# A mask correction of the grouped feed-forward in four bands of 32 rows, with a new table of turns

## The chip, the core and the metric

The kernel runs on one core of one Trainium2 chip. The core has a matrix engine (PE; PEld is its weight loading), a vector engine (DVE), a scalar engine for activations (ACT), a general engine (POOL) and a queue engine that starts most of the transfers (SP). The metric is the device time of one execution, in microseconds (us). Everything is computed in float32.

## The reference

Input `x` has 64 x 64 tokens of 256 numbers, 4096 rows. Two layers are computed, each with a mixer, a cross attention on `ctx_512` and a feed-forward, all with a residual. The change lies in the last of the six parts, the grouped feed-forward of layer 1:

```python
def _L1_ffn_ref(hidden_states, gate_w, mask_up_w, gate_proj_w, up_proj_w, down_proj_w, inv_map):
    scores = jax.nn.softmax(x @ gate_w.T, axis=-1)                  # 64 experts
    topk_w, topk_idx = jax.lax.top_k(scores, 8)
    w_e = jnp.zeros((N, E), x.dtype).at[jnp.arange(N)[:, None], topk_idx].add(topk_w)
    flat = w_e[:, inv_map]                                          # 8 groups of 8
    scalar = flat.sum(-1)
    soft = jax.nn.softmax(jnp.where(flat == 0, NEG_INF, flat), axis=-1)
    xg = x[:, None, :] + jnp.einsum('ngi,ghi->ngh', soft, mask_up_w)
    g = jnp.einsum('ngh,gih->ngi', xg, gate_proj_w)                 # 176 wide, 8 groups
    u = jnp.einsum('ngh,gih->ngi', xg, up_proj_w)
    a = jax.nn.silu(g) * u
    d = jnp.einsum('ngi,ghi->ngh', a, down_proj_w)
    y = jnp.einsum('ng,ngh->nh', scalar, d)
```

The product of `xg` with the gate and up weights is split: `x` times the weights of the group, plus `soft` (8 numbers of each token and group) times `mask_up_w` multiplied by the weights beforehand. The second summand is called the correction here.

## The kernel before

The 4096 rows are 32 tiles of 128; two tiles are a block, so there are 16 blocks. Each part of the network is a stage with one small program (a generator) for each engine and block: `s1` (state space mixer), `s2` and `s3` (latent cross attention), `shared`, `experts` and `more` (mixture of experts, with rows sorted through memory), `s4` (recurrent mixer of layer 1), `s5` (its cross attention), `s6` (the grouped feed-forward, with `ffn` once ahead of it to prepare weights). Where a program says `yield`, its engine may pass to another program. `weave` decides: every piece of every program has a due time, `START` of its stage and block plus its entry in `TURNS`, and the pieces of an engine are written down in the order of these times. That order is fixed when the program is built; each engine then runs its list strictly in order and waits at semaphores. The due times do nothing else.

From about the middle of the program, one period of the list holds `s6` of block n, `s5` of block n + 1 and `s4` of block n + 2. `s4` and `s5` have one set of buffers each, so they run block after block; `s6` has two (`arena` and `BIG`).

The accumulators of PE are eight banks (`ps`). A stage takes them in turn from a ring: `s4` and `s5` from banks 0 to 3 (ring "s5"), `s6` and `ffn` from banks 4 to 7 (ring "s6"). Before PE may write a bank it waits for the step that emptied it last.

What `s6` does with a block, by the lines of the profile:

- L1926 transposes the normalised rows `h` (made by ACT at L872); ACT copies them to `hT` (L2080). L1936 computes the scores, DVE and ACT make a softmax and pick the eight largest (L2012 to L2029), L1944 transposes them, L1953 applies `inv_map`. DVE and ACT make the softmax of each group, which ends with L2052, and L1961 transposes the result; DVE copies it to `soT` (L2055).
- For each of the two tiles and for g = 0 to 3, PE computes two groups, g and g + 4: L1972 multiplies `hT` with the 352 columns of a group (two matmuls for each of the two groups, so four), L1978 adds the correction, one matmul for each group. `soT` has 64 rows, 8 for each group; the correction of group g + 4c takes the band of 32 rows 32c to 32c + 31, of which only 8 count, since `MG` (64 rows x 8 groups x 352) is zero elsewhere. ACT takes the silu of the gate half (L2094), DVE multiplies it with the up half and the group's weight into `AG` (L2064).
- L1988 transposes `AG` in three banks, ACT copies it (L2102), L1997 multiplies with the down weights (11 matmuls), DVE adds the result to `X` (L2069), which frees the bank, and SP stores it (L2112).

Each matmul is issued as two instructions by the compiler, so the four of L1972 are eight in the trace and the two of L1978 are four.

In `s4`, DVE runs two scans (L1524, later L1542 and L1544), a chain of products (L1549 to L1555), a reciprocal (L1557) and a product (L1561); PE multiplies the result with the output weights (L1492), DVE adds that to `X` (L1564). POOL then gathers the rows of the next block (L1611). In `s5`, L1678 are transposes, L1692 and L1706 matmuls on bands of 32 rows that use four banks of ring "s5" at a time, L1717 products whose output is 32 rows wide, L1726 transposes; POOL adds the result to `X` (L1841).

## Time and profile before

| | us |
|---|---|
| median of 3 runs | 2146.43 (2146.39 to 2149.85) |
| the profiled execution's own time | 2144.75 |
| its span, first to last instruction | 2143.0 |
| PE busy | 2039.6 (95%) |
| DVE busy | 1370.2 (64%) |
| ACT busy | 993.2 (46%) |
| POOL busy | 641.0 (30%) |
| mean granted clock of PE | 0.989 |

The span is read in three parts: the first layer up to about 1250 us with the expert stages at its end, the even stretch from 1252 to 2047 us in which `s4`, `s5` and `s6` repeat every 59.1 us, and the end, in which `s6` of the last blocks runs alone.

### The profile page before, as it was taken

What the parts mean: (1) busy time and instruction counts of PE and PEld (TensorE: products, weight loads), DVE (VectorE), ACT (ScalarE), POOL (GpSimd) and SP (SyncE); (2) the same over time, 40 slices, a digit from 0 to 9 for tenths busy, and PEclk for the clock granted to TensorE, in tenths of its full rate; (3) what the DMA queues carried; (4) which work ended last, traced back from release to release, by engine and by line L of the source; (5) the groups of instructions that cost most, each with busy time, mean ns of one, the idle gap of its engine ahead of it and who ended that gap; (6) DMA issues with size and microseconds to landing.
All of it is one profiled execution on the core that took longest, in us unless ns stands there. A gap on an engine that the chain in (4) does not pass through costs nothing.

```text
span 2143.0 us, 40150 instructions
## 1 busy us (share of the span) xinstructions
PE 2039.6 (95%) x15072; PEld 1574.9 (73%) x15072; DVE 1370.2 (64%) x3453; ACT 993.2 (46%) x1974; POOL 641.0 (30%) x988
## 2 busy tenths in 40 slices
PE   6999999999999999999878799999999999999998
PEld 5888888888888778888656566666666666666665
DVE  3677777777778424333256687777777777777631
ACT  1455555555545433333234354455445445454542
POOL 1334443343344620000132332333332333333200
PEclk9999999999999999999899899999999999999999
DMA  5300150000001343222211100000000000000000
GB/s 166 119 14 23 32 194 14 9 21 14 9 21 50 124 150 126 84 80 77 82 49 31 57 23 26 25 26 26 26 13 16 26 26 26 24 26 25 16 6 8
DMA packets 82347, 102.18 MB, mean 48 GB/s; under 512 B 17128, under 2 KB 68464, under 8 KB 81648
## 3 DMA queue, kind: packets, MB, share of 16 engines
q1 hardware_dynamic: 76016, 82.84, 12.1%
q0 software_dynamic: 6144, 16.79, 2.4%
q8 instruction: 125, 2.05, 0.4%
q14 instruction: 62, 0.51, 0.1%
HBM read 62.90 MB, written 36.70 MB: 46 GB/s over the span
## 4 chain that ended last, share of the span: by engine, by line
PE 89%; DVE 4%; ACT 3%; issue 2%; another core or an unknown queue 1%; POOL 1%; DMA 1%; SPq 1%; ACTq 0%; POOLq 0%; DVEq 0%
PE ps L1972 15%; PE ps L1384 9%; PE ps L1997 7%; PE ps L366 7%; PE ps L725 5%; PE ps L782 5%; PE ps L1978 5%; PE ps L1482 4%; PE ps L415 2%; PE ps L1375 2%; PE ps L1988 2%; PE ps L1286 2%; PE ps L1706 2%; PE ps L1692 1%; PE ps L1717 1%
## 5 line engine op out<-in xcount | busy, mean ns | idle before, releaser
L1384 PE MATMUL ps<-BIG,arena 128*128 x912 | 220.4, 390 | 25.1 <-DVE arena L1417 8.6
L1384 PEld LDWEIGHTS ps<-BIG,arena 128*128 128x128 f32 x912 | 170.4, 194 | 56.8 <-issue 35.6
L1420 DVE COPY arena<-ps 128x512 f32<-128x512 f32 x114 | 78.4, 689 | 140.7 <-PE ps L1384 135.4
L1972 PE MATMUL ps<-EARLY,arena 128*128 128x352 f32 x512 | 166.6, 468 | 0.0
L1972 PE MATMUL ps<-EARLY,BIG 128*128 128x352 f32 x512 | 166.5, 468 | 0.0
L366 PE MATMUL ps<-arena,EARLY 128*128 128x256 f32 x640 | 150.7, 385 | 0.0
L1440 ACT ACTIVATE arena<-ps,BIG 128x128 f32<-128x128 f32 x304 | 85.9, 373 | 138.5 <-PE ps L1375 132.8
L1972 PEld LDWEIGHTS ps<-EARLY,BIG 128*128 128x128 f32 x512 | 92.7, 190 | 56.2 <-issue 12.2
L1972 PEld LDWEIGHTS ps<-EARLY,arena 128*128 128x128 f32 x512 | 92.7, 190 | 55.8 <-issue 11.2
L1217 POOL DMA_INDIRECT rows_by_slot<-back,posi x64 | 62.5, 976 | 232.2 <-DMA back<-rows_by_token 214.5
L366 PEld LDWEIGHTS ps<-arena,EARLY 128*128 128x128 f32 x640 | 119.0, 192 | 16.9 <-issue 2.3
L1611 POOL DMA_INDIRECT arena<-results_by_slot,posi x64 | 63.0, 985 | 137.1 <-DVE X L1564 110.8
L468 DVE SCALAR_TENSOR_TENSOR arena<-ps,c_convw,arena 128x252 f32<-128x252 f32 (+2 forms) x192 | 91.4, 476 | 6.8
L2064 DVE SCALAR_TENSOR_TENSOR BIG<-BIG,ps 128x176 f32<-128x176 f32 x128 | 45.0, 393 | 74.6 <-ACT BIG L2094 74.6
L1623 POOL TENSOR_SCALAR arena<-arena,om 128x256 f32<-128x256 f32 x96 | 51.6, 551 | 136.2 <-ACT arena L1575 136.2
L2064 DVE SCALAR_TENSOR_TENSOR arena<-arena,ps 128x176 f32<-128x176 f32 x128 | 45.0, 393 | 71.0 <-ACT arena L2094 71.0
L1482 PE MATMUL ps<-arena,c_w_kvro 128*128 128x256 f32 x384 | 87.7, 385 | 0.0
L1997 PE MATMUL ps<-BIG 128*128 128x256 f32 x352 | 79.6, 382 | 6.4 <-ACT BIG L2102 4.0
L1997 PE MATMUL ps<-BIG,arena 128*128 128x256 f32 x352 | 79.5, 382 | 5.4 <-issue 2.9
L1799 ACT ACTIVATE arena<-ps 128x512 f32<-128x512 f32 x128 | 66.5, 602 | 38.5 <-PE ps L1706 38.4
L570 POOL TENSOR_TENSOR arena<-arena 128x512 f32<-128x512 f32 x32 | 40.6, 1268 | 143.5 <-DVE arena L495 143.5
L1771 DVE TENSOR_REDUCE arena<-ps 128x8 f32<-128x512 f32 x128 | 80.1, 679 | 1.5 <-PE ps L1692 1.4
(404 smaller groups left out, 4823.3 us busy)
## 6 DMA issues: line engine op xcount, KB each, us to landing
arena<-rows_by_slot SPq DMA_DIRECT2D x38, 256.0 KB, 2.7
results_by_slot<-arena SPq DMA_DIRECT2D x38, 256.0 KB, 2.1
rows_by_slot<-zrow SPq DMA_DIRECT2D x3, 2304.0 KB, 15.5
BIG<-in_moe_w SPq DMA_DIRECT2D x3, 1792.0 KB, 9.9
X<-in_x SPq DMA_DIRECT2D x8, 512.0 KB, 4.9
rows_by_token<-BIG SPq DMA_DIRECT2D x16, 256.0 KB
arena<-rows_by_token SPq DMA_DIRECT2D x16, 256.0 KB
back<-rows_by_token SPq DMA_DIRECT2D x16, 256.0 KB
```

The source lines that it names most:

```text
L366: m = e.matmul(ps[:, f * 256:f * 256 + 256], w_in[:, c, c0 + f * P:c0 + f * P + P], L.hT[:, c, :], start=c == 0, stop=c == 1, skip_group_c ...
L468: m = e.scalar_tensor_tensor(c3[:, :, d:64], s3[:, :, 0:64 - d], convw[:, f, 3 - d:4 - d], c3[:, :, d:64], ALU.mult, ALU.add)
L725: m = e.matmul(ps[:, f * 256:f * 256 + 256], Aw[:, c, (2 * g + f) * P:(2 * g + f) * P + P], L.hT[:, c, :], start=c == 0, stop=c == 1, skip ...
L782: m = e.matmul(ps[:, 0:256], L.qT[:, q, i * P:i * P + P], Bw[:, q, :], start=q == 0, stop=q == 7, skip_group_check=True)
L1384: m = e.matmul(ps[:, q * 256:q * 256 + 256], src[:, q, c * P:c * P + P], BIG[:, bass.ds(pe_reg[ex.A.j0 + 2 * n + q] + (w0 + c * 256), 256) ...
L1440: m = e.activation(dst[:, q, c * P:c * P + P], bank.of(k(name))[:, q * 256 + c * P:q * 256 + c * P + P], func, bias=BIG[:, bass.ds(act_reg ...
L1482: m = e.matmul(ps[:, f * 256:f * 256 + 256], kvro[:, j, c, f * P:f * P + P], L.mx[j][:, c, :, :], start=c == 0, stop=c == 1, skip_group_ch ...
L1771: e.tensor_reduce(L.hq[:, i, :, 2 * q:2 * q + 2, 8], bank.of(k(f"s{i}{q}"))[:, :].rearrange("p (g k l) -> p g k l", g=4, k=2), AX, ALU.max ...
L1972: e.matmul(ps[:, 0:352], L.hT[:, q, ts], WG[:, q, gs], start=q == 0, stop=False, skip_group_check=True)
L1978: e.matmul(bank.of(k(f"u{i}{g}{c}"))[:, 0:352], L.soT[rows, ts], MG[rows, gs], start=False, stop=True, skip_group_check=True).then_inc(*ba ...
L1997: m = e.matmul(ps[:, 0:256], L.AT[:, q, :], WD[:, q, :], start=q == 0, stop=q == 10, skip_group_check=True)
L2064: e.scalar_tensor_tensor(L.AG[:, gg * 176:gg * 176 + 176], L.sg[:, c, :], L.s8[0][:, 8 * i + gg:8 * i + gg + 1], bank.of(k(f"u{i}{g}{c}")) ...
```

## The change

1. **Four bands.** `soT` gets 128 rows: four bands of 32 of which 16 count. Band q holds group q in its first 8 rows and group q + 4 in the next 8. Where one tensor operation on DVE wrote the group softmax (L2052), four smaller ones (L2064 of the new file) now write it into a zeroed buffer `so` in this layout. `MG` becomes 128 rows x 2 x 352, and the host lays out `mw` and `mg` to match.
2. **Four groups a batch.** For each tile there are two batches, b = 0 and 1. A batch takes all four banks of the ring "s6" and waits until all four are empty, then issues the four corrections (on four different bands, one bank each, now as the first summand), then the four groups' eight matmuls with `hT`, with a `yield` between groups. Before, the matmuls with `hT` came first and the correction second.
3. **Small groups in the other ring.** The five small results of `s6` (transposed h, scores, transposed weights, `inv_map`, transposed softmax) take banks from ring "s5" in place of "s6".
4. **`sg`** has four buffers in place of two, so ACT may be four groups ahead of DVE.
5. **A new table.** All entries of `START` and `TURNS` are replaced, for every stage and engine, so the lists of all five engines change throughout the program. Two lines of about ninety are shown.

```diff
-    "s6": {"dve": (0.41, 8.37, 8.42, 20.05, 24.63, 27.76, 32.04, 36.9, 37.82, 46.6, 50.4, 64.45, 67.43, 71.67, 75.47,
+    "s6": {"dve": (1.55, 9.29, 10.85, 16.29, 25.86, 28.47, 36.17, 40.9, 42.35, 53.48, 53.48, 66.81, 70.55, 72.67,
...
-        MG = BIG[0:64, 2816:5632]
+        MG = BIG[:, 2816:3520].rearrange("p (b n) -> p b n", b=2)
...
-            ps = bank.take("s6", k("so"), s6v, n, "soT")
+            ps = bank.take("s5", k("so"), s6v, n, "soT")
             e.wait_ge(*s6v.at(n, "so"))
             e.wait_ge(*bank.empty(k("so")))
             for i in range(TB):
-                m = e.transpose(ps[0:64, i * P:i * P + P], L.fl[:, i, :], ident)
+                m = e.transpose(ps[:, i * P:i * P + P], L.so[:, i, :], ident)
             m.then_inc(*bank.made(k("so")))
             for i in range(TB):
                 ts = slice(i * P, i * P + P)
-                for g in range(4):
+                for b in range(2):
                     yield
-                    for c in range(2):
-                        gs = slice((g + 4 * c) * 352, (g + 4 * c) * 352 + 352)
-                        ps = bank.take("s6", k(f"u{i}{g}{c}"), s6v, n, f"ag{i}{g}{c}")
-                        e.wait_ge(*bank.empty(k(f"u{i}{g}{c}")))
-                        for q in range(2):
-                            e.matmul(ps[:, 0:352], L.hT[:, q, ts], WG[:, q, gs], start=q == 0, stop=False,
-                                     skip_group_check=True)
-                    if i == 0 and g == 0:
+                    if i == 0 and b == 0:
                         e.wait_ge(*s6v.at(n, "soT"))
-                    for c in range(2):
-                        rows, gs = slice(32 * c, 32 * c + 32), slice((g + 4 * c) * 352, (g + 4 * c) * 352 + 352)
-                        e.matmul(bank.of(k(f"u{i}{g}{c}"))[:, 0:352], L.soT[rows, ts], MG[rows, gs], start=False, stop=True,
-                                 skip_group_check=True).then_inc(*bank.made(k(f"u{i}{g}{c}")))
+                    for q in range(4):
+                        g = 4 * b + q
+                        bank.take("s6", k(f"u{i}{g}"), s6v, n, f"ag{i}{g}")
+                        e.wait_ge(*bank.empty(k(f"u{i}{g}")))
+                    for q in range(4):
+                        rows, ps = slice(32 * q, 32 * q + 32), bank.of(k(f"u{i}{4 * b + q}"))
+                        e.matmul(ps[:, 0:352], L.soT[rows, ts], MG[rows, b, :], start=True, stop=False,
+                                 skip_group_check=True)
+                    for q in range(4):
+                        if q:
+                            yield
+                        g = 4 * b + q
+                        ps = bank.of(k(f"u{i}{g}"))
+                        for c in range(2):
+                            m = e.matmul(ps[:, 0:352], L.hT[:, c, ts], WG[:, c, g * 352:g * 352 + 352], start=False,
+                                         stop=c == 1, skip_group_check=True)
+                        m.then_inc(*bank.made(k(f"u{i}{g}")))
...
-            e.tensor_tensor(g3(L.fl), g3(L.fl), bc(L.s8[3]), ALU.mult).then_inc(*sig("so"))
+            for i in range(TB):
+                for b in range(2):
+                    m = e.tensor_tensor(L.so[:, i, :].rearrange("p (q w) -> p q w", q=4)[:, :, 8 * b:8 * b + 8],
+                                        L.fl[:, i, 32 * b:32 * b + 32].rearrange("p (q w) -> p q w", q=4),
+                                        L.s8[3][:, 8 * i + 4 * b:8 * i + 4 * b + 4].unsqueeze(2).broadcast_to([P, 4, 8]), ALU.mult)
+            m.then_inc(*sig("so"))
```

In the new file the lines of `s6` are: corrections L1977, matmuls with `hT` L1985, transposes of `AG` L1996, down projection L2005, transposed h L1928, softmax transposes L1963; on DVE the four small products L2064, `soT` L2070, the products into `AG` L2078, the sum into `X` L2083.

How the list of PE changes, one stretch in the middle of the program, from the recurrent mixer's first projections (L1482) on. Before:

```order
L1482 MATMUL ps<-arena,c_w_kvro 128x256 x12
L1997 MATMUL ps<-BIG,arena 128x256 x11
L1961 MATMUL ps<-c_ident,BIG 64x128 x2
L1706 MATMUL ps<-arena 128x256 x8
L1972 MATMUL ps<-EARLY,BIG 128x352 x4
L1978 MATMUL ps<-BIG 128x352 x2
L1972 MATMUL ps<-EARLY,BIG 128x352 x4
L1978 MATMUL ps<-BIG 128x352 x2
L1678 MATMUL ps<-c_ident,arena 128x128 x4
L1717 MATMUL ps<-arena 32x256 x8
L1972 MATMUL ps<-EARLY,BIG 128x352 x4
L1978 MATMUL ps<-BIG 128x352 x2
```

The same stretch in the changed kernel:

```order
L1482 MATMUL ps<-arena,c_w_kvro 128x256 x4
L1996 MATMUL ps<-c_ident,arena 128x128 x3
L1482 MATMUL ps<-arena,c_w_kvro 128x256 x8
L2005 MATMUL ps<-BIG,arena 128x256 x11
L1706 MATMUL ps<-arena 128x256 x8
L1963 MATMUL ps<-c_ident,BIG 128x128 x2
L1678 MATMUL ps<-c_ident,arena 128x128 x4
L1977 MATMUL ps<-BIG 128x352 x4
L1985 MATMUL ps<-EARLY,BIG 128x352 x4
L1717 MATMUL ps<-arena 32x256 x8
L1985 MATMUL ps<-EARLY,BIG 128x352 x4
L1706 MATMUL ps<-arena 128x256 x8
```

The corrections now stand ahead of the first matmul with `hT`, four together, and only one step of transposes (L1678) lies between the transposed softmax (L1963) and them; before, L1706 and four matmuls with `hT` lay there. After the last row shown the next four corrections follow at once.

How the list of DVE changes at the same place, from the last product of the group softmax on. Before:

```order
L2052 TENSOR_TENSOR arena<-arena 128x128
L1542 SCALAR_TENSOR_TENSOR arena<-arena 128x520
L1544 SCALAR_TENSOR_TENSOR arena<-arena 128x520
L2055 COPY arena<-ps 64x256
L2069 TENSOR_TENSOR X<-ps,X 128x256
L2064 SCALAR_TENSOR_TENSOR arena<-arena,ps 128x176 x4
L1549 TENSOR_TENSOR arena<-arena 128x512
L1551 TENSOR_TENSOR arena<-arena 128x512
L1553 TENSOR_TENSOR arena<-arena 128x512
L1555 SCALAR_TENSOR_TENSOR arena<-arena 128x512
L1557 RECIPROCAL arena<-arena 128x512
L1561 TENSOR_TENSOR arena<-arena 128x512
```

The four products of `AG` (L2064) stand between the copy to `soT` and the chain L1549 to L1561.

DVE at the same place in the changed kernel, from the four small products (L2064) on:

```order
L2064 TENSOR_TENSOR BIG<-BIG 128x4x8 x4
L1542 SCALAR_TENSOR_TENSOR arena<-arena 128x520
L1544 SCALAR_TENSOR_TENSOR arena<-arena 128x520
L2083 TENSOR_TENSOR X<-ps,X 128x256
L2070 COPY BIG<-ps 128x256
L1549 TENSOR_TENSOR arena<-arena 128x512
L1551 TENSOR_TENSOR arena<-arena 128x512
L1553 TENSOR_TENSOR arena<-arena 128x512
L1555 SCALAR_TENSOR_TENSOR arena<-arena 128x512
L1557 RECIPROCAL arena<-arena 128x512
L2078 SCALAR_TENSOR_TENSOR BIG<-BIG,ps 128x176 x4
L1561 TENSOR_TENSOR arena<-arena 128x512
```

The copy to `soT` (L2070) stands behind the sum into `X`, and all products of the first batch into `AG` (L2078) stand behind the chain L1549 to L1557.

SP's list changes too. At the start of the program it was, before:

```order
L2116 DMA X<-in_x 128x4x256
L598 DMA arena<-in_wqr 64x768
L598 DMA arena<-in_wkr 64x256
L598 DMA arena<-in_wkcq 96x2x512
L598 DMA arena<-in_wq 128x1024
```

The list begins with `x`, and the loads of L598 follow at once. SP at the start of the changed kernel:

```order
L2141 DMA c_ident<-in_ident 128x128
L2141 DMA EARLY<-in_w_in 128x2568
L2141 DMA c_nscale<-in_nscale 128x2
L2141 DMA c_convw<-in_convw 128x16
L2141 DMA c_convb<-in_convb 128x4
```

The tables and the first layer's weights now come first; the loads of L598 and the rest of `x` stand behind them.

## Rows read from the trace of the kernel before

**Rows 1.** Two stretches: length, busy time (instructions) by engine, PE's clock, DMA.
```profile
1000.00:1250.00 250.00, 204.47 (x1234) 153.72 (x1233) 139.53 (x251) 91.39 (x220) 68.90 (x93) 0.91 0.17 56
1252.00:2047.00 795.00, 783.60 (x5887) 539.04 (x5889) 592.28 (x1302) 400.29 (x763) 245.83 (x357) 1.00 0.07 23
```

**Rows 2.** PE in time order: start us, length, line, count, [idle before it].
```profile
1637.44 0.38 PE L1961 MATMUL ps<-c_ident,BIG 128*64 128x128 f32 x2
1637.76 1.15 PE L1706 MATMUL ps<-arena 32*128 32x256 f32 x16
1638.83 2.63 PE L1972 MATMUL ps<-EARLY,BIG 128*128 128x352 f32 x8
1641.40 0.86 PE L1978 MATMUL ps<-BIG 32*128 32x352 f32 x4
1642.19 2.63 PE L1972 MATMUL ps<-EARLY,BIG 128*128 128x352 f32 x8
...
1645.54 0.66 PE L1678 MATMUL ps<-c_ident,arena 128*128 128x128 f32 x4
1646.13 1.07 PE L1717 MATMUL ps<-arena 128*32 128x256 f32 x16
...
1654.70 1.99 PE L1492 MATMUL ps<-c_w_kvro,arena 128*128 128x256 f32 x8
...
1669.47 0.66 PE L1926 MATMUL ps<-c_ident,arena 128*128 128x128 f32 x4 [0.99 <-ACT arena L872]
...
1686.78 0.55 PE L1988 MATMUL ps<-c_ident,BIG 128*128 128x128 f32 x3
1687.16 5.35 PE L1482 MATMUL ps<-arena,c_w_kvro 128*128 128x256 f32 x24
...
1697.10 0.38 PE L1961 MATMUL ps<-c_ident,arena 128*64 128x128 f32 x2
```

**Rows 3.** DVE in time order, the end of the softmax and the chain of `s4`.
```profile
1645.99 0.71 DVE L2064 SCALAR_TENSOR_TENSOR BIG<-BIG,ps 128x176 f32<-128x176 f32 x2 [2.64 <-ACT BIG L2094]
1646.62 0.68 DVE L1549 TENSOR_TENSOR arena<-arena 128x512 f32<-128x512 f32 x1
...
1653.60 0.69 DVE L1561 TENSOR_TENSOR arena<-arena 128x512 f32<-128x512 f32 x1
...
1689.91 1.23 DVE L1524 TENSOR_TENSOR_SCAN arena<-td,arena 128x520 f32<-128x520 f32 x1
...
1695.31 0.89 DVE L2052 TENSOR_TENSOR arena<-arena 128x128 f32<-128x128 f32 x1
...
1700.44 0.39 DVE L2055 COPY arena<-ps 64x256 f32<-64x256 f32 x1
1700.76 0.40 DVE L2069 TENSOR_TENSOR X<-ps,X 128x256 f32<-128x256 f32 x1
```

**Rows 4.** Two short steps of DVE one behind the other, in time order.
```profile
1724.94 0.17 DVE L429 TENSOR_SCALAR small<-small 128x2 f32<-128x2 f32 x1
1725.02 0.16 DVE L808 TENSOR_SCALAR small<-small 128x2 f32<-128x2 f32 x1
```

**Rows 5.** POOL in time order, beside the end of the softmax.
```profile
1694.87 1.19 POOL L1631 TENSOR_TENSOR arena<-arena 128x512 f32<-128x512 f32 x1 [2.07 <-DVE arena L1537]
1696.01 1.23 POOL L1634 TENSOR_TENSOR arena<-arena 128x512 f32<-128x512 f32 x1
```

**Rows 6.** From L1492 to the next block's h, in another period, on PE.
```profile
1714.35 1.99 PE L1492 MATMUL ps<-c_w_kvro,arena 128*128 128x256 f32 x8
...
1728.56 0.66 PE L1926 MATMUL ps<-c_ident,BIG 128*128 128x128 f32 x4
```

**Rows 7.** ACT in the same period, where h is made.
```profile
1726.62 1.09 ACT L872 ACTIVATE BIG<-X,small 128x256 f32<-128x256 f32 x2 [6.22 <-POOL small L882]
```

**Rows 8.** PE at the start of the program, in time order.
```profile
11.90 2.82 PE L609 MATMUL ps<-arena 64*96 64x64 f32 x16 [11.90 <-DMA c_ident<-in_ident]
...
22.08 3.68 PE L628 MATMUL ps<-arena 96*128 96x64 f32 x16 [5.46 <-DVE arena L645]
```

229 lines of the change are left out of this document (117 added, 112 removed), and 9 rows, old and new, of the table START.

## The prediction, made before the run

> **What bounds the kernel now.** The first view is the busy time of the engines over the whole span, shown in the table above: PE has work for 95% of it. The second is the same by stretches [rows 1]. From 1252 to 2047 us PE is busy 783.6 of 795 us, DVE 592.3; PE is idle 11.4 us, some 0.85 in each period of 59.1. So in this stretch only less time of PE's own instructions can shorten the span, and only as long as the change makes PE wait no longer than it saves. From 1000 to 1250 us PE is busy 204.5 of 250, with a granted clock of 0.91, and 45.5 us are idle: a stretch of waits. The third view is PE in order of time [rows 2]: there the price of a correction can be read. The fourth is DVE and POOL in order of time [rows 3 to 5], which shows when the inputs of the corrections are ready.
>
> **Fewer, wider corrections.** A step of eight instructions of L1972 and four of L1978 takes 1642.19 - 1638.83 = 3.36 us [rows 2]. The eight alone: from the start of L1482 to that of L1961 stand 24 instructions of L1482 and 22 of L1997 with 256 columns each, 46 in 1697.10 - 1687.16 = 9.94 us, so 0.216 each, 0.297 for 352 columns, 2.38 for eight. That leaves 0.98 for a visit to the bands. Two passes of 352 columns are 0.59 of it, the other 0.39 goes to changing over and back. The visit already has its two bands side by side; one behind the other, four instructions would be 1.19 alone, more than the 0.79 between L1978's start and the next line's start (1641.40 to 1642.19).
>
> That four bands can also run side by side is shown by L1706: 16 instructions of 256 columns on four bands stand 1638.83 - 1637.76 = 1.07 us before the next line [rows 2]. One behind the other they would take 16 x 0.216 = 3.5. So I take 0.98 for a visit of four corrections too. A block has eight visits before and four after: 3.9 us less. In places a visit now follows L1706 directly, whose changeover it shares, as it sometimes did; I take off 0.3 and have 3.6 for a block, 58 us for 16 blocks. The bounds of the visit's price are 0.98 and, if bands ran two at a time, 0.98 + 0.59 = 1.57.
>
> As a sentence apart: the Trainium skill, TensorEngine Tiling (Array Packing), section Gotcha 1: PSUM Pressure, says that row tiles running at once need different banks of PSUM; by that rule the new code's four banks a batch are the price of the overlap, and L1706, whose row agrees with it, pays it already. What the rule says against this change is in the next part, worked out from rows.
>
> **What the four banks cost.** The batch needs `soT` and all four banks of its ring before its first correction; before, matmuls with `hT` on two banks came first. I lay the new order of PE over the times of the old. Zero is the start of L1482.
>
> *First batch.* DVE before, after zero: L1524 starts at +2.75 (1689.91 - 1687.16), L2055 at +13.28, and `soT` is ready at +13.67 [rows 3]. PE reached the correction 9.94 + (1641.40 - 1637.44) = 13.9 after zero [rows 2]: no slack. Now four small products replace L2052 (0.89). Their price no row has: the nearest rows are two short steps that start 0.08 apart and last 0.17 [rows 4], so about 0.45 for four; 1.3 if each takes what a step of DVE with PSUM takes (about 0.3). I take 0.45, since each writes 32 numbers a row. The first of two sums into `X` now stands ahead of the copy: 0.32 from L2055 to L2069's start [rows 3] is the pitch of such steps. So `soT` is ready at 13.67 - 0.44 + 0.32 = 13.55. PE now arrives at 9.94 + 0.38 (three transposes moved in, 1687.16 - 1686.78) + 1.07 (L1706) + 0.32 (L1963) + 0.59 (L1678) = 12.3 [rows 2]. It waits 1.3, which before was covered by a step of L1972.
>
> *Second batch.* It needs the first batch's four products out of PSUM, and these now stand behind the chain L1549 to L1557 and ahead of L1561: 1653.60 - 1646.62 = 6.98 for the chain, then 4 x 0.315 (1646.62 - 1645.99 for two) [rows 3]. From 13.55 that gives 21.8. PE arrives after 0.98 + 2 x 2.38 + 1.0 (L1717) + 1.07 (L1706) = 7.8 to 8.1, at 21.6: a wait of 0.2, but nothing is left over. Behind it 0.8 and, in most blocks, two groups of 1.19 stand ahead of L1492, which starts at 25.1. It was 9.94 + (1654.70 - 1637.44) = 27.2 before [rows 2].
>
> *To the next h.* From L1492 it went 14.2 to L1926 on PE, and 1726.62 + 1.09 - 1714.35 = 13.4 to the end of `h` on ACT [rows 6, 7]. PE's own work there is now 13.0 at most, so the chain over DVE, POOL and ACT decides: 13.5, with a wait of 0.5 to 1.0 (0.99 stood there in one period before [rows 2]).
>
> *From there to zero.* 1687.16 - 1669.47 = 17.7 before [rows 2]. Off go three steps of 3.36 and the moved transposes 0.38; on come two visits of 0.98 and eight groups of 1.19, 11.5 together, and an estimated 0.3 for the last batch, whose four banks must be emptied by ACT and DVE (one product, 0.315) while only short transposes cover it: 19.1.
>
> The period is then 25.1 + 13.5 + 19.1 = 57.7 in place of 59.1: 1.4 less. Of the 3.6 won, 2.2 return as waits. Some 14 periods are of this kind, 19.6 us; in the last two blocks, where `s6` has nothing beside it, the four-bank wait is bare, and I take 1 us for both together.
>
> **Small groups in the other ring, four buffers `sg`.** Both only move waits; no instruction is added. The ring of `s5` had free turns beside them, and ACT ahead of DVE helps where DVE is late. Nothing, within 0.2 a block either way.
>
> **Copies and host layout.** `L1963` puts out 128 rows in place of 64 and L2070 copies 128 in place of 64: columns set the time, the same. Zeroing `so` is twice in the whole program, on POOL (30% busy in the table).
>
> **The new table, first layer and experts.** I followed the orders of PE, DVE, ACT and POOL from the start to 1250 us: the places with short cover (expert stages) are as many and of about the same size in both. I take nothing. The bounds: better than half of the 45.5 us idle [rows 1] gone, -25; as much as a third more, +15. At the start of SP's list, `c_ident` and the first weights now come first, and the loads of L598 stand behind fifteen others. PE's start at 11.90 may slip to 16 or 18, but the 5.46 us which L628 waited for L645 go with it, since it is then loaded in between [rows 8]. Nothing, within 4. The stores of `s5` and `s6` come later on SP; nobody waits for them but the end, and they are short beside the last block's.
>
> **The sum.** 2144.75 - 19.6 - 1 = 2124.2 for the profile's own time. The median of the runs is 1.7 above that execution, so 2126 is the median forecast.
>
> **Rivals.**
>
> A. *The forecast*, 2126: visits at 0.98, 2.2 a block back as waits. Its own spread, from the products at 1.3 (0.9 a block later, 12 us) to waits of half the size (15 us less): 2111 to 2138.
>
> B. *The waits are covered.* If DVE gets to `soT` and the products earlier, since `s4` and `s5` now run at another offset, only the sum of PE's work counts: 58 less, 2088. For it: DVE is free a quarter of the time [rows 1]. Against it: `soT` had no slack before, and the chain from L1524 on has not become shorter.
>
> C. *The new table removes waits of the expert stages*: half of the 45.5 us more, 2126 - 24 = 2102. Against it: the orders look alike there.
>
> D. *Slower: the chain on DVE decides the period.* The place is the end of the softmax and L1549 to L1561. L2052 took 0.89 for 128 numbers a row, where L2069, for 256, took 0.40 [rows 3]; POOL's L1631 and L1634 ran beside it, 1.19 and 1.23 [rows 5]. If each small product or the chain L1549 to L1555 is held by one of these, DVE comes 1.5 to 2.4 later to `soT` and to the products of the first batch. PE has no slack at either, so every microsecond beyond the forecast's counts: from 1.4 on the gain is gone, at 2.2 the period is 59.9, and 14 periods make it 2157.
>
> As a sentence apart: the Trainium skill, SBUF, State Buffer, section Who interferes with whom, says that DVE and GpSimd share a pair of ports under an exclusive lock; by that, D's wait is real, and the long L2052 beside POOL fits it, though it happened before the change as well and is in the old period.
>
> E. *The bands run two at a time.* 0.59 more a visit, 2.4 a block, of which about 0.7 is taken from the waits that stand behind a visit (the second batch, L1926): period 57.7 + 1.7 = 59.4, 14 x 1.7 = 24 more than A, 2150. Against it stands L1706 [rows 2].
>
> **How the numbers follow.** A 0.52, B 0.18, C 0.10, D 0.13, E 0.07. The range leaves out the far side of B and D: from 2086, just under B, to 2152, which takes in E and the mild part of D. A change under 0.2% (4.3 us) is about what a measurement can't tell from none: faster 0.77 (A, B and C, 0.80, less 0.03 for A with the first layer's bound of +15 on top), same 0.10 (E and that), slower 0.13 (D).
>
> **What would show it.** In the changed profile: L1977, eight instructions, 0.8 to 0.9 us before L1985, and not 1.4 (A against E). PE idle about 1.3 us ahead of L1977, put down to DVE's L2070, and a little ahead of the second, put down to L2078 (A against B). A period of 57.7 between starts of L1482's groups; 59.9 with L2064 or L1555 stretched beside L1631 and L1634 is D, 55.5 is B. Idle time of PE from 1000 to 1250 of 45 us; 22 is C. The forecast is wrong above all if the table shifts `s4` against `s6` so that the softmax ends earlier than the old times say.

## The result, and the profile after it

The changed kernel is slower. Its median is 2165.2 us (8 runs, 2155.2 to 2172.6) beside 2147.1 for the kernel before on the same chip, ratio 1.0083 (95% interval 1.0070 to 1.0095). The forecast was 2126 with a range up to 2152, so both the size and the sign are wrong. The profiled execution has a span of 2163.0 us, 20.0 more than before.

The page of the changed kernel, busy time by engine, answers to the table ahead of the prediction:

```profile
PE 2012.1 (93%) x15072; PEld 1572.0 (73%) x15072; DVE 1388.7 (64%) x3501; ACT 1005.2 (46%) x1974; POOL 645.4 (30%) x990
```

PE has 27.5 us less work and the span is 20 us longer, so PE stands idle 47 us more. The stretches of [rows 1] in the changed kernel (length, busy time of PE, PEld, DVE, ACT, POOL, PE's clock, DMA):

```profile
1000.00:1250.00 250.00, 203.56 (x1262) 157.47 (x1262) 144.63 (x252) 92.39 (x227) 55.38 (x75) 0.95 0.17 54
1252.00:2047.00 795.00, 746.63 (x5732) 526.39 (x5730) 589.29 (x1323) 405.97 (x754) 257.61 (x371) 0.99 0.08 23
```

In the even stretch idle time of PE went from 11.4 to 48.4 us. The starts of L1482's sixteen groups tell where the 20.0 us arise. The fourth group, the first beside `s6`, starts at 1286.7 in place of 1272.6: 14.1 us are lost ahead of it. From there to the sixteenth it is 720.1 in place of 710.0: 10.1 more. From the sixteenth to the end it is 156.2 in place of 160.4: 4.2 less.

One period of PE in the changed kernel, in order of time (start us, length, line, count, [idle before it]), answers to [rows 2]:

```profile
1707.36 1.99 PE L1482 MATMUL ps<-arena,c_w_kvro 128*128 128x256 f32 x8
...
1719.72 0.41 PE L1963 MATMUL ps<-c_ident,arena 128*128 128x128 f32 x2 [0.76 <-ACT arena L1799]
1720.21 0.63 PE L1678 MATMUL ps<-c_ident,arena 128*128 128x128 f32 x4
1721.59 0.87 PE L1977 MATMUL ps<-BIG,arena 32*128 32x352 f32 x8 [0.75 <-DVE arena L2070]
1722.39 2.63 PE L1985 MATMUL ps<-EARLY,arena 128*128 128x352 f32 x8
1724.95 1.07 PE L1717 MATMUL ps<-arena 128*32 128x256 f32 x16
1725.95 2.63 PE L1985 MATMUL ps<-EARLY,arena 128*128 128x352 f32 x8
1728.52 1.15 PE L1706 MATMUL ps<-arena 32*128 32x256 f32 x16
1729.68 0.87 PE L1977 MATMUL ps<-BIG,arena 32*128 32x352 f32 x8
...
1732.95 1.89 PE L1492 MATMUL ps<-c_w_kvro,arena 128*128 128x256 f32 x8
...
1742.04 5.02 PE L2005 MATMUL ps<-BIG,arena 128*128 128x256 f32 x22 [1.42 <-ACT arena L2115]
1747.14 0.66 PE L1928 MATMUL ps<-c_ident,BIG 128*128 128x128 f32 x4
...
1757.59 0.87 PE L1977 MATMUL ps<-BIG,arena 32*128 32x352 f32 x8 [0.28 <-DVE arena L2078]
...
1766.51 1.99 PE L1482 MATMUL ps<-arena,c_w_kvro 128*128 128x256 f32 x8
```

Three things are to be seen. First, eight instructions of L1977, on four bands, hold PE for 1722.39 - 1721.59 = 0.80 us; four of L1978, on two bands, held it 0.79 in [rows 2]. The four bands do run side by side. Second, the waits named in the prediction are there (L1977 behind L2070, and 0.28 behind L2078), with one that it did not have: 1.42 before L2005, on the copies L2115 of ACT. In the twelve periods from the fourth group to the sixteenth this wait is 1.17 to 1.91, 20.2 us in all. Third, this period, 59.15 us, is as long as one of before. Longer ones come from the clock. Two neighbouring periods, by the same columns as above, and then the place in another period where the clock fell:

```profile
1407.00:1468.00 61.00, 57.28 (x436) 40.43 (x435) 44.82 (x101) 30.64 (x58) 19.50 (x28) 0.97 0.06 18
1468.00:1527.00 59.00, 55.73 (x435) 39.17 (x434) 44.66 (x101) 30.73 (x58) 19.51 (x28) 1.00 0.07 19
```

```profile
1897.36 0.41 PE L1963 MATMUL ps<-c_ident,BIG 128*128 128x128 f32 x2 [0.76 <-ACT arena L1799]
...
1899.16 0.87 PE L1977 MATMUL ps<-BIG 32*128 32x352 f32 x8 [0.69 <-DVE BIG L2070]
1899.97 4.33 PE L1985 MATMUL ps<-EARLY,BIG 128*128 128x352 f32 x8
```

Eight instructions of L1985 took 4.33 in place of 2.63: part of them ran at 1.2 in place of 2.4 GHz, after two waits close together. Five of twelve periods have a fall of the clock, at about 1.6 us each; the kernel before has none between 1252 and 2047 (its clock is 1.00 in [rows 1]). The falls have two places. Two of the five (1542 and 1900 us) stand behind these two waits; the other three (1323, 1443 and 1982 us) begin inside L2005, just behind its own wait of 1.9. A second execution of the changed kernel, `after_again`, has seven, five at the first place and two at the second.

### The profile page after: what moved, and what is told of

It is laid out like the page before. It is cut to its first block, busy times and chain, and to the rows that moved or that the text cites. A ratio compares the mean times of both kernels' runs of the same rounds, so it can differ in the third digit from the quotient of the medians.

```text
span 2163.0 us, 40298 instructions
## 1 busy us (share of the span) xinstructions
PE 2012.1 (93%) x15072; PEld 1572.0 (73%) x15072; DVE 1388.7 (64%) x3501; ACT 1005.2 (46%) x1974; POOL 645.4 (30%) x990
## 3 DMA queue, kind: packets, MB, share of 16 engines
q8 instruction: 126, 2.06, 0.4%
## 4 chain that ended last, share of the span: by engine, by line
PE 73%; DVE 16%; ACT 4%; issue 3%; POOL 2%; another core or an unknown queue 1%; DMA 1%; SPq 0%; ACTq 0%; POOLq 0%; DVEq 0%
PE ps L1985 15%; PE ps L1384 9%; PE ps L366 6%; PE ps L725 4%; PE ps L782 4%; PE ps L2005 3%; PE ps L1977 2%; PE ps L1375 2%; PE ps L415 2%; PE ps L1482 2%; PE ps L1286 2%; PE ps L1996 2%; PE ps L1692 1%; DVE arena L1527 1%; PE ps L1717 1%
## 5 line engine op out<-in xcount | busy, mean ns | idle before, releaser
L1384 PEld LDWEIGHTS ps<-BIG,arena 128*128 128x128 f32 x912 | 168.8, 192 | 59.6 <-issue 38.7
L1985 PE MATMUL ps<-EARLY,BIG 128*128 128x352 f32 x512 | 169.1, 475 | 0.0
L1985 PE MATMUL ps<-EARLY,arena 128*128 128x352 f32 x512 | 166.1, 468 | 0.0
L1611 POOL DMA_INDIRECT arena<-results_by_slot,posi x64 | 63.3, 988 | 310.7 <-DVE X L1564 169.4
L1985 PEld LDWEIGHTS ps<-EARLY,BIG 128*128 128x128 f32 x512 | 94.5, 193 | 63.2 <-issue 22.4
L1985 PEld LDWEIGHTS ps<-EARLY,arena 128*128 128x128 f32 x512 | 92.9, 190 | 61.7 <-issue 19.8
L366 PEld LDWEIGHTS ps<-arena,EARLY 128*128 128x128 f32 x640 | 120.6, 194 | 20.3 <-issue 4.2
L1217 POOL DMA_INDIRECT rows_by_slot<-back,posi x64 | 62.6, 978 | 126.7 <-DMA back<-rows_by_token 81.2
L2108 ACT ACTIVATE BIG<-ps 128x176 f32<-128x176 f32 x128 | 39.4, 317 | 123.5 <-PE ps L1985 123.2
L2005 PE MATMUL ps<-BIG 128*128 128x256 f32 x352 | 83.0, 394 | 12.2 <-ACT BIG L2115 10.4
L2005 PE MATMUL ps<-BIG,arena 128*128 128x256 f32 x352 | 81.2, 387 | 11.9 <-ACT arena L2115 11.9
L1482 PE MATMUL ps<-arena,c_w_kvro 128*128 128x256 f32 x384 | 91.7, 391 | 0.0
L2005 PEld LDWEIGHTS ps<-BIG 128*128 128x128 f32 x352 | 68.4, 197 | 24.0 <-ACT BIG L2115 12.3
L2108 ACT ACTIVATE arena<-ps 128x176 f32<-128x176 f32 x128 | 39.1, 317 | 99.6 <-PE ps L1985 99.4
L2005 PEld LDWEIGHTS ps<-BIG,arena 128*128 128x128 f32 x352 | 67.3, 193 | 23.1 <-ACT arena L2115 13.9
```

Source lines behind the costliest of these rows:

```text
L366: m = e.matmul(ps[:, f * 256:f * 256 + 256], w_in[:, c, c0 + f * P:c0 + f * P + P], L.hT[:, c, :], start=c == 0, stop=c == 1, skip_group_c ...
L1384: m = e.matmul(ps[:, q * 256:q * 256 + 256], src[:, q, c * P:c * P + P], BIG[:, bass.ds(pe_reg[ex.A.j0 + 2 * n + q] + (w0 + c * 256), 256) ...
L1482: m = e.matmul(ps[:, f * 256:f * 256 + 256], kvro[:, j, c, f * P:f * P + P], L.mx[j][:, c, :, :], start=c == 0, stop=c == 1, skip_group_ch ...
L1985: m = e.matmul(ps[:, 0:352], L.hT[:, c, ts], WG[:, c, g * 352:g * 352 + 352], start=False, stop=c == 1, skip_group_check=True)
L2005: m = e.matmul(ps[:, 0:256], L.AT[:, q, :], WD[:, q, :], start=q == 0, stop=q == 10, skip_group_check=True)
L2108: e.activation(L.sg[:, g % 4, :], bank.of(k(f"u{i}{g}"))[:, 0:176], ACT.Silu).then_inc(*sig(f"sg{i}{g}"))
```

## The experiments

Each group below ran on one chip together with the kernel before, and each of the five groups on another chip. That kernel took 2147.1, 2147.8 and 2150.9 us in three groups, and 2131.6 and 2131.5 in two others. I call these the slower and the faster condition; whether it is the chip or something about it that changes, no run here tells. The result above is of the slower condition. Ratios are always to the kernel before in the same group.

### Which part of the program loses: the first pair, a faulty one

The idea was to cross the tables: old turns up to the first `s6` with the new `s6`, and the other way round.

```
START/TURNS of s1, s2, s3, prod, first, x, tables, scatter, shared, experts, more, ffn; START of s4[0:2], s5[0]: from the other kernel
all later START: shifted by 201.96
```

> The changed kernel, but with the old table for every stage up to the end of the first layer, the first two blocks of s4, the first of s5, and ffn; from the first s6 on the lists are those of the changed kernel. Theory (two thirds of the loss lie in the new table ahead of s6, not in the four bands): the fourth group of L1482 starts near 1273 us in place of 1286.7, and the time is about 13 us under the changed kernel's, 2152. Rival (the first layer came out late by its clock in that one execution, or the loss is made by the batches): within 4 us of the changed kernel, 2161 to 2169.

> The counterpart: the kernel before, with the new table for the same stages, and its own lists from the first s6 on. Theory: the new table ahead of s6 costs the same here, so about 13 us over the kernel before, 2160. Rival: no change, 2147.

Measured: 2194.5 us (ratio 1.0230, 1.0209 to 1.0251) and 2189.0 (1.0195, 1.0175 to 1.0215). Both are far slower than either kernel. The fourth group of L1482 comes at 1310.6 and 1315.3 us, 38 and 29 us later than in the kernel whose table stands ahead (1272.6 and 1286.7). About 20 of this arise between the first and the third group (distances 75.2 and 72.6 us, and 78.0 and 72.0, in place of 67.3 and 62.6 in the kernel before and 64.9 and 63.2 in the changed one), most of the rest already ahead of the first. The cross was bad: blocks 0 and 1 of `s4` and block 0 of `s5` lie among the expert stages, and had the turns of the one table with the starts of the other. Neither the theory nor the rival is tested by it. It says only that a mismatch there costs 30 to 40 us, and that from the fourth group on each kernel keeps its own periods (60.2 on average with the new `s6`, 59.2 with the old).

### Covering the wait for soT, and doubling the visits

`cover` issues the matmuls with `hT` of two groups ahead of the four corrections:

```diff
-   take and wait for four banks; four corrections; hT for g0, g1, g2, g3
+   wait for two banks; hT for g0, g1; wait for soT and the other two banks; four corrections; hT for g2, g3
```

> The changed kernel with another order inside a batch: the matmuls with hT of the first two groups first, as the kernel before had it, then the four corrections, then the other two groups. Theory (the wait for soT ahead of the corrections costs 0.7 us a period by itself, and the falls of the clock that follow such waits cost another 1.7 in about every third): the wait before L1977 goes, the falls in the even stretch go, the period is 58.0 to 58.5, and the time is 14 to 20 us lower, 2146 to 2151. Rival (the chain L1549 to L1561 on DVE decides, so that the wait only moves to the second batch's banks): the period stays at 59.2 and the time within 5 us of the changed kernel less its clock falls, 2155 to 2165.

Measured: 2144.0 us (0.9988, 0.9977 to 0.9999). The place of the wait, in its PE list:

```profile
1471.61 2.53 PE L1979 MATMUL ps<-EARLY,arena 128*128 128x352 f32 x8
1474.08 0.87 PE L1990 MATMUL ps<-BIG,arena 32*128 32x352 f32 x8
...
1492.68 5.02 PE L2011 MATMUL ps<-BIG,arena 128*128 128x256 f32 x22 [1.87 <-ACT arena L2121]
```

The corrections (L1990 there) no longer wait, and the periods without a fall are 58.2 to 58.7, apart from two of 59.5 and 59.7 in which PE also waits 1.0 to 1.2 before L1928. Two falls are left in place of five, at 1730 and 1965 us, both inside L2011, behind its wait. So the theory held for the wait and nearly for the period; its falls did not all go, and the time is 2 us below its range. The rival, by which DVE's chain L1549 to L1561 would only take the wait over, fell. The wait on the copies of ACT (L2011 here is L2005) stayed, at 1.2 to 1.9.

`pairs` keeps everything but issues the corrections two and two:

```diff
-   C0 C1 C2 C3 | hT g0, g1, g2, g3
+   C0 C1 | hT g0, g1 | C2 C3 | hT g2, g3
```

> The changed kernel with its four corrections of a batch issued two and two: two ahead of the first two groups, two ahead of the others; banks, waits and tables unchanged, so eight visits to the bands a block in place of four. If a visit costs 0.98 alone (0.59 of passes and 0.39 of changing over), four more are 3.9 a block less what the waits take up: period 61.5 to 62.5, time 2200 to 2215. If what matters is the number of changes between bands and whole columns (eight more, at 0.1 each, and 0.59 of passes four times), 3.2 a block: 2195 to 2205. If four bands had run two at a time, only the changes are added, 1.6 a block: 2185.

Measured: 2213.3 us (1.0311, 1.0292 to 1.0330), periods without a fall of 62.0 to 62.6, apart from two of 63.8 with a longer wait before L1928. Against 59.2 that is about 3.0 for four more visits, but the wait before L2005 (L2006 here) has also fallen, from 1.2 to 1.9 down to 0.7 to 1.0 where no wait before L1928 stands. PE's busy time in a period without a fall rose by 3.5, from 55.6 to 59.1. The rows say how this is made up. A new visit next to another step on bands, such as the one behind L1717, adds the 0.79 that it holds PE. One between full-width steps also lengthens both neighbours: where L1985's twelve instructions held PE 1763.77 - 1760.12 = 3.65 in the changed kernel, the same twelve with a visit between them hold it 1597.91 - 1593.28 = 4.63 here, 0.98 more. Two of the four new visits are of each kind, 3.5 together. The first of the three expected outcomes held, in period and time: the prediction's 0.98 is right for a visit by itself, and one beside a step on bands costs 0.2 less. Two bands cost what four do.

### The cross again, joined cleanly

The first two blocks of `s4` and the first of `s5` now take the turns of the same table as their starts, so that the five lists are exactly those of one kernel up to the first step of `s6` and those of the other from there on.

```diff
-   (START[stage][n], TURNS[stage][engine], program(n))
+   (START[stage][n], (FIRST if n < {"s4": 2, "s5": 1}.get(stage, 0) else TURNS)[stage][engine], program(n))
```

> The changed kernel, whose five lists are those of the kernel before up to the first step of s6 (all stages of the first layer, s4 of blocks 0 and 1 and s5 of block 0 with their own old turns this time) and its own from there on. Theory (about 9 to 14 us of the loss lie in the new table ahead of s6): the fourth group of L1482 starts at 1273 to 1276 in place of 1286.7, the even stretch is as in the changed kernel (60.0 a period on average), time 2151 to 2156. Rival (only the clock of that execution made it late): 2161 to 2168.

> The counterpart: the kernel before with the changed kernel's lists up to the first step of s6, its own from there on. Theory: fourth group of L1482 at 1282 to 1287, then periods of 59.1, time 2156 to 2161. Rival: 2147.

Measured: 2129.6 us (0.9986, 0.9973 to 0.9999) and 2130.8 us (1.0000, 0.9985 to 1.0015). This group was the first in the faster condition. Neither theory nor rival foresaw it: the new `s6` is a little faster here, and the new table ahead costs nothing (fourth group of L1482 at 1265.0, with the old table 1270.2). The instructions last as long as before. What is shorter are waits: in `old_table_ahead`, which has the new `s6`, PE waits before L2005 0.36 us in every period, most periods are 58.0 to 58.2, and one fall of the clock is left, behind the wait for `soT`. The changed kernel itself was never run in the faster condition.

### Two numbers of the table, and one

`so_early` moves L1963 ahead of L1706 on PE and L2070 ahead of L2083 on DVE.

```diff
-   "s6": {"dve": (..., 28.47, 36.17, ...)    "pe": (..., 23.47, 35.14, ...)
+   "s6": {"dve": (..., 28.47, 33.3, ...)     "pe": (..., 23.47, 32.2, ...)
```

> The changed kernel with two numbers of the table moved: the transposes of the softmax (L1963) ahead of L1706 in PE's list, so that their bank in the ring of s5 is no longer one that ACT (L1799) has to empty first, and the copy to soT (L2070) ahead of the sum into X (L2083) in DVE's. Theory (both waits end at the same place, DVE's scans L1542 and L1544, which stand between the softmax and the copy): the 0.76 wait of L1963 goes, the wait of L1977 grows to 1.1 to 1.3, soT is ready 0.3 earlier, period 58.9, time 2160 to 2164. Rival (the wait of L1963 is a cost of the ring by itself): period 58.4, time 2152 to 2156.

Measured: 2191.7 us (1.0275, 1.0252 to 1.0298); theory and rival both wrong. Its waits of PE between 1300 and 2000 us (total, times, longest):

```profile
PE ps L1706 <- DVE arena L2070: 19.4, 6, 3.2
PE ps L1706 <- DVE BIG L2070: 16.1, 5, 3.2
PE ps L1678 <- ACT arena L1799: 8.0, 11, 0.7
```

L1706 needs all four banks of the ring, and one of them now holds the transposed softmax until L2070 has copied it. So with this group in `s5`'s ring there are only two orders. Behind L1706 it waits 0.76 for ACT to empty the first of the four banks; ahead of it, L1706 waits 3.2. So the move into the other ring does bring a wait of its own; what it costs in sum is tested by `cover_so` below.

`gather_late` moves POOL's gathers behind the sums into `X` and the powers for `h`.

```diff
-   "s4": {"pool": (-47.93, -30.43, ...
+   "s4": {"pool": (-30.9, -30.43, ...
```

> The changed kernel with one number of the table moved: POOL's four indirect gathers (L1611) behind the sums into X and the small powers for h (L879, L882), not ahead of them. Theory (while POOL issues the gathers, ACT answers PE's signals 0.4 us late and more, which makes the copies L2115 late and L2005 wait 1.2 to 1.9 us): the wait before L2005 falls to 0.4 or less, the period by 1.0 to 1.5, time 2148 to 2154, unless the next block of s4, whose rows come later, then waits for them. Rival (L2115 is late because of its place in ACT's list): the wait of L2005 stays at 1.2 or more and the time within 4 us of 2165.

Measured: 2263.8 us (1.0605, 1.0577 to 1.0633). It says nothing on its question. It ran in the faster condition, where L2005 waits 0.4 anyway, and the rows of `s4` came so late that PE waited up to 8.1 us in each period for DVE, before L1977.

### What differs between the conditions

In the faster condition the same step of the list can be laid beside the changed kernel's. ACT and POOL of the changed kernel, slower condition:

```profile
1739.31 0.60 ACT L1804 ACTIVATE arena<-ps 128x512 f32<-128x512 f32 x1 [1.75 <-PE ps L1717]
1740.03 1.96 ACT L2115 ACTIVATE arena<-ps 128x512 f32<-128x512 f32 x3
```

```profile
1737.25 0.97 POOL L1611 DMA_INDIRECT arena<-results_by_slot,posi  x1 [0.30 <-issue]
1738.52 0.95 POOL L1611 DMA_INDIRECT arena<-results_by_slot,posi  x1 [0.30 <-issue]
1739.77 0.95 POOL L1611 DMA_INDIRECT arena<-results_by_slot,posi  x1 [0.30 <-issue]
```

The same step with the same lists in `old_table_ahead`, faster condition, ACT, POOL and PE:

```profile
1711.93 0.60 ACT L1804 ACTIVATE arena<-ps 128x512 f32<-128x512 f32 x1 [1.15 <-PE ps L1717]
1712.48 1.47 ACT L2115 ACTIVATE arena<-ps 128x512 f32<-128x512 f32 x3
```

```profile
1711.73 0.95 POOL L1611 DMA_INDIRECT arena<-results_by_slot,posi  x1 [0.30 <-issue]
1712.98 0.95 POOL L1611 DMA_INDIRECT arena<-results_by_slot,posi  x1 [0.30 <-issue]
```

```profile
1710.79 1.07 PE L1717 MATMUL ps<-arena 128*32 128x256 f32 x16
...
1714.01 5.02 PE L2005 MATMUL ps<-BIG,arena 128*128 128x256 f32 x22 [0.36 <-ACT arena L2115]
```

PE starts L1717 at 1710.79 and ACT's L1804 follows 1.14 later, as the sixteen matmuls end. In the changed kernel L1717 starts at 1737.58 and L1804 only 1.73 later; the three copies then take 1.96 in place of 1.47. This happens while POOL issues the indirect gathers, and the gathers are the same in both conditions. The theory formed here: in the slower condition ACT and DVE answer PE late while POOL issues an indirect transfer, and the new table puts more work that PE waits for beside such transfers.

Two things in the traces make this theory sharper. First, it is PE's signals alone that come late. Beside the same gather, DVE answers ACT at once in the changed kernel:

```profile
1737.25 0.32 ACT L2108 ACTIVATE arena<-ps 128x176 f32<-128x176 f32 x1 [0.87 <-PE ps L1985]
1737.60 0.40 DVE L2078 SCALAR_TENSOR_TENSOR arena<-arena,ps 128x176 f32<-128x176 f32 x1 [0.79 <-ACT arena L2108]
```

ACT's step ends at 1737.57 and DVE's starts 0.03 later. Take the signals that ended a wait between 1252 and 2047 us, and the time of the semaphore event in this trace. 26 signals of PE come 0.4 to 1.27 us behind the recorded end of their matmul, two in each period (L1717, then L1726 or L1996), all beside the gathers or just behind them. All other signals of PE come within 0.05, and every signal of ACT and DVE within 0.02. In `old_table_ahead`, with the same gathers, no signal of PE is later than 0.05. The ends of matmuls are modelled in a profile, so whether PE works slower there or only signals later, these rows don't tell.

Second, the place matters within one execution. In the kernel before, slower condition, two neighbouring periods:

```profile
1659.74 1.08 POOL L1611 DMA_INDIRECT arena<-results_by_slot,posi  x1 [0.16 <-issue]
1660.31 5.01 PE L1997 MATMUL ps<-BIG 128*128 128x256 f32 x22 [0.36 <-ACT BIG L2102]
...
1717.36 1.08 POOL L1611 DMA_INDIRECT arena<-results_by_slot,posi  x1 [8.09 <-DVE X L1564]
1720.46 5.02 PE L1997 MATMUL ps<-BIG,arena 128*128 128x256 f32 x22 [0.86 <-ACT arena L2102]
```

Where the first gather starts 2.7 us behind L1717 (1657.06), the copies are nearly done and L1997 waits 0.36; where it starts 0.65 behind L1717 (1716.71), L1997 waits 0.86. In the changed kernel the first gather starts at 1735.86, 1.7 ahead of L1717, and the whole chain from L1717 to the copies lies beside the four.

The next group tests the theory by taking the indirect gathers away:

```diff
-   e.indirect_dma_start(y[:, i * 256:i * 256 + 256], None, ys_d[n // CUT], idx)
+   e.dma_start(y[:, i * 256:i * 256 + 256], ys_d[n // CUT][fixed row : fixed row + 128, :])
```

> The changed kernel itself once more, because the two mixed tables came out on a run of the kernel before at 2131.6 us in place of 2147.1, with every instruction as long as before and shorter waits. Theory (the chips differ: on the first one ACT and DVE answer PE 0.3 to 0.9 us late while POOL issues an indirect gather, L1611, on the other in 0.04 to 0.07; the change moves such gathers beside work that PE waits for): where the kernel before takes 2147, the changed one takes 1.008 of it, where it takes 2132, the ratio is 0.998 to 1.002. Rival (chance in the clock falls alone made the first ratio): the same ratio everywhere, near 1.000 to 1.002.

> The changed kernel in which POOL's four indirect gathers of a block of s4 (L1611) are plain transfers of the same 128 x 256 numbers from fixed rows of the same memory, started by POOL at the same places (so the rows are not the ones the experts made). Theory (the indirect gather makes ACT and DVE answer late): on a chip of the first kind the waits of L2005 fall from 1.2 to 1.9 down to 0.4, some clock falls go, and the even period comes to 58.1 to 58.5; on one of the second kind nothing but 0.3 us a period. Rival (L2115 is late by its place in the list): L2005 waits the same as in the changed kernel on the same chip.

> The same exchange in the kernel before. Theory: its waits before L1997, 0.36 to 0.9 on the first chip, fall to 0.36, so 0.5 a period and 7 us on a chip of the first kind, and nothing on one of the second. Rival: no change on either.

Measured, slower condition, kernel before 2147.8: the changed kernel 2167.0 (1.0087, 1.0073 to 1.0101), so the first ratio stands. With plain gathers 2138.0 (0.9954, 0.9939 to 0.9969), 29.0 us less. The kernel before with plain gathers 2142.8 (0.9974, 0.9965 to 0.9983), 5.0 us less. So on one chip the change costs 19.2 us with the gathers and gains 4.9 without them. (The plain gathers read rows that the experts did not make for them; the amounts and places are the same.) The same period in `plain_after`, PE, and one whole period:

```profile
1702.98 0.87 PE L1977 MATMUL ps<-BIG,arena 32*128 32x352 f32 x8 [0.84 <-DVE arena L2070]
...
1722.18 5.02 PE L2005 MATMUL ps<-BIG,arena 128*128 128x256 f32 x22 [0.36 <-ACT arena L2115]
1727.43 0.66 PE L1928 MATMUL ps<-c_ident,BIG 128*128 128x128 f32 x4 [0.23 <-ACT BIG L872]
```

```profile
1688.70:1746.80 58.10, 55.54 (x436) 39.15 (x435) 44.49 (x101) 30.67 (x58) 17.32 (x28) 1.00 0.08 24
```

L2005 waits 0.36 in every period, there is no fall of the clock between 1252 and 2060, the periods are 58.0 to 58.2, and no signal of PE is late any more. The rival (the place in ACT's list) fell: the place is the same. The wait for `soT` stayed, at 0.7 to 0.8, so it alone makes no fall here. Plain gathers also hold POOL for less time (2.2 us in place of 5), but that is not what shortens the periods: in the faster condition `old_table_ahead` issues the same indirect gathers, and its periods are 58.0 to 58.2 too, except four of 59.0 to 59.5.

`cover_so` keeps the gathers. It has the order of `cover` and L1963 in a bank of the ring "s6":

```diff
-   ps = bank.take("s5", k("so"), s6v, n, "soT")
+   ps = bank.take("s6", k("so"), s6v, n, "soT")
```

> The order of the run that covered the wait for soT (two groups of matmuls with hT, the four corrections, the other two groups), and the transposed softmax (L1963) in a bank of the ring of s6 in place of s5's, all tables as in the changed kernel. Theory (L1963's wait of 0.76 is the ring's: the bank behind the four of L1706 is one that ACT's L1799 must empty; in the s6 ring the batch waits for soT anyway): the wait of L1963 goes and nothing takes its place, because the corrections now stand 2.4 us later; period 0.7 lower than with the s5 ring, 57.3 to 57.8 where there are no clock falls; 0.990 to 0.994 of the kernel before. Rival (the wait moves on to L1977 or to the bank that s5 takes next): the period stays at 58.3 to 58.5, ratio 0.998.

Measured: 2140.3 us (0.9970, 0.9958 to 0.9982), the lowest ratio of a kernel that keeps its indirect gathers. The wait of L1963 is gone, but the periods without falls are 58.0 to 58.7 and two of 59.4 and 59.6, as with `cover`: the next step, L1678, now waits 0.39 for the same L1799, the corrections up to 0.5 for `soT`, and L2005 (L2011 here) 1.4 to 1.9 as ever. The rival, that the wait moves on, held; the theory fell.

### Ahead of s6

> The changed kernel with the old lists up to the first step of s6, once more, for a chip on which the kernel before takes 2147 us and ACT and DVE answer late beside POOL's gathers. Theory (on such a chip the new table ahead of s6 costs 8 to 14 us, above all by falls of the clock near 740 and 783 us): fourth group of L1482 at 1272 to 1276, time 2151 to 2157. Rival (the first stages cost nothing on either chip, all of the 19 us lies in the even stretch): 2163 to 2168. On a chip of the second kind: 2129 to 2131 again.

> The kernel before with the changed kernel's lists up to the first step of s6. Theory on a chip of the first kind: 2155 to 2161, with the falls of the clock near 740 and 783 us. Rival: 2147. On one of the second kind: 2131 again.

> The changed kernel with plain transfers in place of POOL's indirect gathers (L1611) and of its indirect scatters of the first layer (L1217), the same amounts at the same places. Theory (the falls of the clock near 740 and 783 us, among the scatters, come from late answers beside them too): these falls are gone, the fourth group of L1482 comes at 1268 to 1274 in place of 1282, the time is 8 to 12 us under the run with plain gathers alone, 0.990 to 0.992 of the kernel before. Rival (the falls belong to the order of the new table): fourth group at 1282, ratio 0.995.

> Both that the runs point to: the order that covers the wait for soT, with L1963 in the ring of s6 (ratio 0.997 with the new table), and the old lists up to the first step of s6. If the new table ahead costs 8 to 14 us on a chip of the first kind: 0.990 to 0.993 of the kernel before, 2127 to 2133. If it costs nothing: 0.997. On a chip of the second kind: 0.995 to 0.999.

`plain_both` exchanges L1217 as well as L1611, so that it leaves out the sorting of rows altogether. `old_ahead_2` and `new_ahead_2` are the same kernels as `old_table_ahead` and `new_table_ahead`. Measured, slower condition, kernel before 2150.9: `old_ahead_2` 2172.4 (1.0083, 1.0064 to 1.0101), `new_ahead_2` 2162.2 (1.0049, 1.0032 to 1.0066), `plain_both` 2120.2 (0.9853, 0.9836 to 0.9870), `best` 2148.4 (0.9981, 0.9971 to 0.9991).

The same two kernels thus take 2172.4 and 2162.2 us here and 2129.6 and 2130.8 in the faster condition. The new lists ahead of `s6` cost the kernel before 11 us, as the theory said (fourth group of L1482 at 1287.9). Taking them from the changed kernel gave nothing back: `old_ahead_2` is above the range of its theory and of its rival, its even stretch is longer (728.3 us from the fourth to the sixteenth group in place of 720.1, with eight falls of the clock in place of five), and `best`, also above its theory's range, is no better than `cover_so` (their intervals overlap). So the two parts do not add up, and why not is open. The place of the fourth group is no firm measure in this condition either. With the old lists ahead it came at 1272.6, 1277.0 (`plain_before`), 1284.4 and 1285.2 us, with the new ones at 1275.8 (`cover_so`) to 1287.9. The 14.1 us between the first two traces are therefore not all the table's.

What stands on firmer ground is `plain_both`, which went further than its theory (1268 to 1274, ratio 0.990 to 0.992): without any indirect transfer the fourth group comes at 1264.8, against 1282.2 in `plain_after`, whose scatters are indirect. PE from 725 to 750 and from 775 to 800 us, in the changed kernel and then in `plain_both` (length, PE busy, clock, DMA):

```profile
725.00:750.00 25.00, 21.44 (x205) 0.80 0.27 86
775.00:800.00 25.00, 22.09 (x78) 0.73 0.54 184
```

```profile
725.00:750.00 25.00, 22.53 (x185) 1.00 0.32 107
775.00:800.00 25.00, 23.70 (x137) 1.00 0.42 139
```

In the changed kernel PE stops there for 0.3 to 1.1 us again and again (L742 and L770, with nothing named as the cause but issue), while POOL issues a row of scatters. The 64 instructions of a block of L742 take 5.0 us there, from 734.81 on, and 1.16 in `plain_both`:

```profile
736.60 0.34 PE L742 MATMUL ps<-BIG 64*64 64x64 f32 x5 [0.37 <-issue]
737.32 0.36 PE L742 MATMUL ps<-BIG 64*64 64x64 f32 x5 [0.38 <-issue]
738.05 0.35 PE L742 MATMUL ps<-BIG 64*64 64x64 f32 x4 [0.37 <-issue]
739.47 0.21 PE L742 MATMUL ps<-BIG 64*64 64x64 f32 x1 [1.08 <-issue]
```

```profile
736.47 0.96 POOL L1217 DMA_INDIRECT rows_by_slot<-back,posi  x1 [0.30 <-issue]
737.74 0.96 POOL L1217 DMA_INDIRECT rows_by_slot<-back,posi  x1 [0.30 <-issue]
```

The clock falls right behind. This is the same lateness seen at PE itself: between 715 and 800 us six traces of the slower condition with indirect scatters (`before`, `after`, `after_again`, `cover_so`, `plain_after`, `new_ahead_2`) have 1.5 to 4.1 us of such stops, and `new_table_ahead` (indirect scatters, faster condition) and `plain_both` and `plain_both_2` have none. The falls near 740 and 783 us are gone in `plain_both`; in `plain_both_2` one short fall is left near 777, and `cover_so`, with its scatters, has none near 783, so not every one of these falls hangs on the scatters. The rival, that they belong to the order of the table, fell.

### Both kernels without indirect transfers

> The kernel before with plain transfers in place of all of POOL's indirect ones (L1217 and L1611), the counterpart of plain_both. Theory (the change would be faster by 0.3 to 0.7% if nothing made ACT and DVE answer late, and the indirect transfers take 20 us more from the changed kernel than from the one before): about 2129 us, 0.990 to 0.993 of the kernel before, fourth group of L1482 near 1270, periods of 58.6. Rival (the indirect transfers cost both alike, and the changed kernel gains 1.5% only by leaving them out): 0.983 to 0.986, as plain_both.

> The changed kernel with plain transfers in place of all of POOL's indirect ones, once more, so that it stands on the same chip as its counterpart. Theory: 0.985 to 0.987 of the kernel before, 0.993 to 0.997 of plain_both_before, from the period (58.0 against 58.6, 7 us) and the first layer (5 us). Rival: the same time as plain_both_before.

Measured, in the faster condition (kernel before 2131.5): the kernel before without indirect transfers 2129.2 (0.9983, 0.9971 to 0.9996), the changed kernel without them 2119.4 (0.9951, 0.9933 to 0.9969). Both ratios are above those expected, because these had been set against a kernel before of the slower condition; the time of about 2129 us, the period of 58.6 and the ratio of the two kernels held. The change is then worth 2129.2 - 2119.4 = 9.9 us, 0.5% faster. In the traces 704.1 us from the fourth to the sixteenth group become 696.4, so 7.7 (58.7 a period become 58.0), 4.3 are gained behind it, and 3.9 are lost ahead of it. And the changed kernel without indirect transfers takes 2120.2 us in the slower condition and 2119.4 in the faster: for it the two conditions are one.

In the slower condition the sums are then: the kernel before loses about 2147.8 - 2129.2 = 19 us to the indirect transfers, the changed kernel 2167.0 - 2119.4 = 48. The difference, 29, against the 10 won, is the 19 us by which it came out slower. (The 2129.2 is from the other condition; the changed kernel's twin agrees between both to 0.8.) Most of the 29 is the gathers' part, 29.0 against 5.0 on one chip, and that lies in the even stretch, which came down from 723.6 us (`after_again`) to 696.6 (`plain_after`). The scatters' part is 17.8 against 13.6, across chips.

## Why the prediction was wrong, point by point

The forecast had 19.6 us less in the even stretch, 1 less at the end and nothing ahead; the traces have 10.1 more, 4.2 less and 14.1 more. Three steps failed. The stretch from L1492 to the next h was put at 13.5 a period, decided by `h`, with no wait before L2005: that wait came to 20.2 us over twelve periods, and to 4.3 without the indirect gathers, because PE's signals to ACT come late beside them. Falls of the clock were put at nothing: five came, about 8 us, and none without the gathers. The new table ahead of `s6` was put at nothing: the kernel before loses 11 us with it in the slower condition. The even stretch is 720.1 us with the gathers, 696.6 without; twelve forecast periods are 692.4. So 23.5 of the 27.7 us missed there belong to the gathers and 4.2 to the terms below. The forecast also counted 14 periods where the traces have twelve between the fourth and the sixteenth group.

- **PE bounds the even stretch.** Right for what the lists ask; but see the last points.
- **Four bands run side by side.** Right: 0.80 for a visit of four corrections, 0.79 for one of two. Rival E fell.
- **3.6 us less of PE's work a block.** Mis-sized: it is 2.5 to 2.6. Taken from start to start without the waits, one period of `plain_before` holds 58.2 us of work and one of `plain_after` 55.7. The visits themselves went from 5.9 to 3.2 and the matmuls with `hT` from 20.3 to 19.9, 3.0 together, where the forecast had 3.6: one of the eight visits before ran interleaved with L1706 and held PE only about 0.3. Some 0.4 came back in steps that now have other neighbours (0.26 in the down projection, 0.18 in L1963, 0.10 in L1482). The 0.98 for a visit was right where it stands between full-width steps, as `pairs` shows: eight instructions of L1985 hold PE 1737.05 - 1734.68 = 2.37 with a full-width step on either side, as assumed, and 1728.52 - 1725.95 = 2.57 with steps on bands on both.
- **Four small products at 0.45.** Wrong by more than the upper bound. From L2064's start to L1542's it is 2.06 us. The count of durations (least, median, most, in ns) shows why:

```profile
L2064 DVE TENSOR_TENSOR arena<-arena x32: 178/185/1221, 1236.0 to 2069.7; 128x32 f32<-128x32 f32 x32
```

  Three of four take 0.18 as assumed, one 1.2: it stands beside POOL's L1631 or L1634, as L2052 did with 0.89. Part of it is given back behind: L1542 starts later and holds DVE 1718.64 - 1717.49 = 1.15, where before it held it 1698.26 - 1696.12 = 2.14. This was rival D's mechanism, and its rows were shown; the step that failed was to take the low value because of the size of the product, when the price was that of the neighbour. The Trainium skill, SBUF — State Buffer, section Who interferes with whom, says that a DVE instruction with two inputs in SBUF contends with a GpSimd instruction that reads SBUF; the 1.2 us agree.
- **The wait for `soT`, 1.3.** Near in sum, 0.76 before L1963 and 0.75 before L1977, but partly by luck: the first half is a wait for ACT's L1799 in the other ring, which the forecast did not have, and the copy was ready at +14.2 in place of +13.55.
- **The second batch 0.2, the last 0.3.** Near: nothing at the second, 0.28 at the last.
- **The small groups in the other ring, nothing.** The wait of L1963 is the ring's, but taking it away (`cover_so`) moved it on by one step. Nothing in sum, by luck.
- **From L1492 to the next h, 13.5 decided by `h`.** Wrong: 1747.14 - 1732.95 = 14.2, decided by the late L2005. Without the gathers it is 1727.43 - 1714.35 = 13.1, and there L1928 does wait for `h`, 0.23.
- **The period, 57.7.** It is 59.0 to 59.6 with the gathers where no fall comes (once 60.2), and 58.0 without. Of 2.6 us of work less, 2.0 return as waits (0.36 a period before, 2.4 after, both without gathers), where the forecast had 2.2. So the waits were well judged once the late signals are away. That 57.7 is within 0.3 of 58.0 is luck all the same: the work saved was put 1.0 too high, and the 59.1 from which it was taken held 0.5 of late signals; without them the period before was 58.6. The structural gain is 0.6, not 1.4.
- **Falls of the clock.** Left out of the forecast. Five of them, about 8 us: three behind the long wait of L2005 and two behind the waits for `soT`. Without the gathers there are none. They are not bound to late signals alone, though: `old_table_ahead` has one behind the wait for `soT` with L2005 at 0.36.
- **The new table ahead of s6, nothing, within -25 and +15.** 14 in the first pair of traces, 11 by `new_ahead_2`, 0 in the faster condition, 4 without indirect transfers. Under the new `s6` the old lists gave nothing back. The step that failed was to read the cost off the number of places with short cover; that what stands on POOL beside them makes the rest of it is likely from L742, but the experiments do not separate it. At the start of the program the forecast held: L742 begins at 99.8 in place of 96.4 us, within the 4.
- **The end, 1 us.** 4.2, under-sized.

The slower rival D was given 0.13 and would have ended near this time (2157), but by DVE's chain in each period; the time came from elsewhere.

## What to carry to other kernels

A list order is worth what stands beside it on other engines, and not only what waits for it: look where POOL issues indirect transfers, and keep steps of PE whose results ACT or DVE must hand back soon out of those microseconds (`gather_late` shows that moving the gathers instead can cost more, 132 us). When a price is read from a row that is longer than its size explains, as L2052's 0.89, carry the neighbour's price to whatever replaces it. When a kernel waits more or longer, count the granted clock: here two waits of 0.7 us close together, or one of 1.9, were followed by a fall that cost about 1.6 more in five of twelve periods. And run a kernel on more than one chip before you trust a difference of 1%: the same list, `old_ahead_2`, is 0.8% slower than the kernel before on one and 0.1% faster on another.

## What the runs showed of the hardware

- While POOL issues indirect transfers (about 0.96 us each, 1.27 apart), PE's signals to ACT and DVE come up to 0.6 us (kernel before) and 1.3 us (changed kernel) behind the recorded end of the matmul in one condition, and within 0.05 in the other. Signals of ACT and DVE come within 0.02 in both. A row of 64 small matmuls beside the scatters took 5.0 us in place of 1.16. Plain transfers started by POOL at the same place (four in 2.2 us) do not do this. The kernel before took 2147 to 2151 us in the one condition and 2131.5 in the other; the changed kernel without indirect transfers 2120.2 and 2119.4. The section of the Trainium skill named above says that PE and ACT never wait on anyone; that is said of ports, and whether a port has a part in this lateness no run here shows. What makes the two conditions differ is open.
- Eight matmuls on four bands of 32 rows hold PE 0.80 us where four on two bands hold it 0.79. A full-width step beside them is 0.10 longer on each side that touches a step on bands (2.37, 2.47 and 2.57 for eight matmuls of 352 columns).
